# The end of a graph kernel: four tables of sums in HBM are added onto sums in SBUF, by Pool's accumulating transfers instead of loads and adds

## The chip, the cores and the metric

The kernel runs on one core of a Trainium2 chip. The metric is the device time of one execution in microseconds; the time before is the median of three runs. "PE" is TensorE, "DVE" is VectorE, "ACT" is ScalarE, "Pool" is GpSimd and "SP" is SyncE, which here only issues transfers.

## The reference

One layer of a graph network over 6250 nodes with 64 features and 200,000 edges. `h` is the node matrix after a layer norm and a Relu. Each edge makes a message, the messages are summed by their source node, divided by the node's count of edges, and a second small network makes the update:

```python
h = jnp.maximum(_layernorm(x, axis=-1), 0.0)
msg = jnp.concatenate([h[col], edge_attr], axis=1)
msg = jnp.maximum(msg @ W1a + b1a, 0.0) @ W1b + b1b
summed = jax.ops.segment_sum(msg, row, num_segments=x.shape[0])
counts = jax.ops.segment_sum(jnp.ones((row.shape[0],), msg.dtype), row, num_segments=x.shape[0])
agg = summed / jnp.maximum(counts, 1.0)[:, None]
out = jnp.maximum(jnp.concatenate([h, agg], axis=1) @ W2a + b2a, 0.0) @ W2b + b2b
return x + out
```

The kernel moves `W1b` behind the sum (the product `W1b @ W2a` is made once, in `wcq`), so what is summed by node is the Relu of the first layer, 64 numbers and a count of 1: `W` = 65 words a node. With 50 nodes on each of 128 partitions (`NT` = 50) a whole set of sums is 128 x 3250 words, 1625 KB.

## The kernel before

**Two kinds of edges.** Part of the edges goes the "sparse" way: groups of six tiles of 128 edges are combined and written to one of four tables in HBM, `sums[0]` to `sums[3]`, by Pool's indirect accumulating transfers (`scatter`, L626), 650 tiles in all. Tile after tile takes the next table, up to tile `OPEN` = 638; the last twelve take tables 0 and 1 only (`KEPT` = 2), so that tables 2 and 3 are complete early. A scatter waits until the one before it on the same table has landed. The other edges go the "dense" way: PE routes them to buckets and sums them by node (`route`, `sum_nodes`, L1563), and DVE adds each half result from PSUM to `dense` in SBUF (`add_sums`, L1139). The dense sums of a macro step are made in ten adds, each of five columns of nodes, in order from column 0 to 49; the semaphore `summed` counts them over the whole program (230 = 23 macro steps of ten). Only the last ten set when `dense` is final.

**The end before the change.** SP waits until tables 2 and 3 are complete (`table_done`, L532), loads table 3 whole into `xc` (`early_tab`, L533) and table 2 whole into `area` (`tab[2]`, L535). Then it waits for Pool's last scatters (`sums_done`) and for the tenth of the last dense adds, and loads tables 0 and 1 in five chunks of columns (`CHUNKS`, L544), into `tab[0]` and `tab[1]`. DVE adds the early table to `dense` in five adds behind its last dense add (`add_early`, L1147). Pool adds `tab[1]` and `tab[2]` to `tab[0]` turn by turn (L766, L768).

**The turns.** What is left runs in 13 turns (`NTURNS`) of four nodes a partition, 256 words wide. `pipelined` writes the stages of each engine out in an order that is fixed: a stage with lead 3 works on the turn three ahead of the last stage. For a turn DVE adds `dense` to the tables' sum (`add_dense`, L1407), takes the count (`counts`, L1411), its reciprocal (`inverse`, L1416), the mean (`mean_of`, L1422), later the hidden sum (`hidden_sum`, L1429) and the result (`result`, L1433). PE turns the mean (L1689), multiplies it (L1695, L1697), brings the sign of the counts to the other layout (`met_t`, L1704) and makes the output rows (`out_rows`, L1711). ACT copies and applies Relu (L896, L900), makes the sign (`met_rows`, L906) and the bias of nodes that have edges (`base`, L912). SP stores the results in three parts (L563, L564).

The hidden sum waits for `base`, `base` for PE's `met_t`; each engine works in its written order, so that a stage that waits holds up all behind it on its engine.

A general branch of the program serves inputs that don't fit these windows. The profile has no instruction of it.

## Time and profile before

| | us |
|---|---|
| median of three runs | 1448.33 (1445.06 to 1450.76) |
| profiled execution | 1445.55 |
| its span, first to last instruction | 1443.7 |
| PE busy in the span | 1347.3 (93%) |
| DVE busy | 1340.7 (93%) |
| Pool busy | 1107.6 (77%) |
| ACT busy | 858.9 (59%) |

The span lies inside the execution's own time and is 1.85 us shorter. Busy shares are means over the whole span; at the end, from about 1398 us, the picture is another one, and there a timeline (instructions of one engine in order of start, with the idle time before them in brackets and what released them) tells more than a share.

### The profile page before, as it was taken

The page shows a single profiled execution, that of the slowest core. Times are in us where ns is not written, and L with a number is a line of the kernel's source. Part 1 is how long each engine was busy: PE and PEld are TensorE (multiplying, and loading weights), DVE is VectorE, ACT ScalarE, POOL GpSimd, SP SyncE. Part 2 cuts the span into 40 slices and gives each one's busy share as a digit, 9 for nine tenths or more (in the row PEclk, how much of TensorE's full clock was granted, in tenths as well). Part 3 has the DMA queues.
Part 4 walks back from the last instruction along what each step waited for, and adds up shares of the span by engine and source line. Part 5 has one row for each costly group of instructions (what it writes and reads, how often), then busy time and mean ns, then how long its engine had stood idle before and what let it go on. Part 6 is the DMA issues. An engine that isn't in the chain of part 4 may idle for free. (4 is left out here: it accounts for less than half of the span.)

```text
span 1443.7 us, 66451 instructions
## 1 busy us (share of the span) xinstructions
PE 1347.3 (93%) x27502; PEld 1295.7 (90%) x27502; DVE 1340.7 (93%) x4194; ACT 858.9 (59%) x1853; POOL 1107.6 (77%) x737
## 2 busy tenths in 40 slices
PE   1667899999999999999999999999999999999967
PEld 1456899999999999999999999999999999999965
DVE  6889899999999899999999999999999999999877
ACT  2427566666666666666666566656666666666605
POOL 3527888887888878887788868888688887888744
PEclk9589999999999999999999999999999999999989
DMA  7737566776677657776677757776677776767352
GB/s 223 269 70 148 101 117 118 126 124 116 118 127 127 112 113 128 123 133 101 125 126 125 125 103 128 122 128 118 114 131 118 120 127 118 117 122 121 48 146 74
DMA packets 224935, 178.59 MB, mean 124 GB/s; under 512 B 149616, under 2 KB 191726, under 8 KB 223479
## 3 DMA queue, kind: packets, MB, share of 16 engines
q1 hardware_dynamic: 130324, 145.66, 38.2%
q0 software_dynamic: 94304, 28.63, 27.8%
q8 instruction: 218, 3.57, 1.0%
q14 instruction: 89, 0.73, 0.2%
HBM read 140.88 MB, written 33.31 MB: 121 GB/s over the span
## 5 line engine op out<-in xcount | busy, mean ns | idle before, releaser
L626 POOL DMA_INDIRECT sums<-vv,sidx x648 | 1045.3, 1613 | 275.2 <-issue 180.5
L854 ACT ACTIVATE area<-rank_ps 64x392 bf16<-64x392 f32 x1150 | 563.9, 490 | 140.7 <-PE rank_ps L1549 115.3
L1563 PE MATMUL rank_ps<-area 128*128 128x65 bf16 x17250 | 625.6, 193 | 7.1 <-issue 4.1
L1563 PEld LDWEIGHTS rank_ps<-area 128*128 128x128 bf16 x17250 | 597.4, 98 | 23.8 <-issue 10.7
L1549 PE MATMUL rank_ps<-r_d,oh 128*128 128x196 bf16 x4600 | 495.8, 249 | 16.2 <-DVE oh L1117 7.3
L1549 PEld LDWEIGHTS rank_ps<-r_d,oh 128*128 128x128 bf16 x4600 | 380.1, 96 | 29.4 <-issue 8.3
L1132 DVE TENSOR_SCALAR area<-iota,local 128x640 bf16<-128x640 int16 x1150 | 393.2, 406 | 4.1
L1117 DVE TENSOR_SCALAR oh<-iota,rank 128x640 bf16<-128x640 int16 x920 | 310.9, 407 | 7.2 <-PE rank_ps L1549 5.7
L831 ACT ACTIVATE r_d<-z_ps 128x512 f32<-128x512 f32 x247 | 147.6, 597 | 78.4 <-PE z_ps L1519 73.4
L842 ACT ACTIVATE vv<-c_ps 128x396 f32<-128x396 f32 x108 | 54.1, 501 | 226.9 <-PE c_ps L1538 225.2
L1139 DVE TENSOR_TENSOR dense<-rank_ps,dense 128x325 f32<-128x325 f32 x230 | 112.1, 487 | 45.5 <-PE rank_ps L1563 44.9
L1513 PE MATMUL z_ps<-wts,et_d 128*128 128x128 f32 x920 | 132.3, 287 | 0.0
L1085 DVE TENSOR_TENSOR r_s<-r_s 128x384 f32<-128x384 f32 x216 | 119.9, 555 | 3.7
L1074 DVE TENSOR_SCALAR same<-ids_s,srcf 128x128 bf16<-128x128 int16 x648 | 118.6, 278 | 0.0
L1513 PEld LDWEIGHTS z_ps<-wts,et_d 128*128 128x128 f32 x920 | 113.4, 194 | 0.0
L1513 PE MATMUL z_ps<-wts,et_s 128*128 128x128 f32 x648 | 100.3, 291 | 1.2 <-issue 1.0
L1513 PEld LDWEIGHTS z_ps<-wts,et_s 128*128 128x128 f32 x648 | 82.5, 194 | 2.0 <-issue 1.6
L1538 PE MATMUL c_ps<-r_s,same 128*128 128x64 bf16 (+1 forms) x1944 | 81.2, 193 | 2.7 <-issue 1.4
L831 ACT ACTIVATE r_s<-z_ps 128x384 f32<-128x384 f32 x108 | 52.8, 489 | 44.8 <-PE z_ps L1519 43.8
L1538 PEld LDWEIGHTS c_ps<-r_s,same 128*128 128x128 bf16 x1944 | 68.3, 97 | 5.0 <-issue 3.8
L1096 DVE TENSOR_TENSOR r_d<-r_d 128x512 f32<-128x512 f32 x98 | 67.2, 685 | 1.7
L1067 DVE TENSOR_SCALAR hots_s<-ids_s,basew 128x384 bf16<-128x384 int16 x216 | 65.1, 342 | 0.9 <-issue 0.8
(193 smaller groups left out, 769.5 us busy)
## 6 DMA issues: line engine op xcount, KB each, us to landing
ids_s<-ids SPq DMA_DIRECT2D x216, 192.0 KB
et_d<-in_e_t SPq DMA_DIRECT2D x115, 256.0 KB
ids_d<-ids SPq DMA_DIRECT2D x115, 256.0 KB
et_s<-in_e_t SPq DMA_DIRECT2D x108, 192.0 KB
sums<-vv,sidx POOLq DMA_INDIRECT x648
sums<-dense POOLq DMA_DIRECT2D x4, 1657.5 KB
wp_s<-p_table SPq DMA_DIRECT2D x216, 15.8 KB
wp_d<-p_table SPq DMA_DIRECT2D x115, 15.8 KB
```

Source lines behind the costliest of these rows:

```text
L626: nc.gpsimd.indirect_dma_start(out=sums[t][:, :], out_offset=bass.IndirectOffsetOnAxis(ap=index, axis=0), in_=rows, in_offset=None, comput ...
L831: nc.scalar.activation(rows3(kind, g)[:, :, PARTS[r]:PARTS[r] + D], z, ACT.Relu).then_inc(split_ready[kind], 1)
L854: ins = nc.scalar.activation(routed[on, t.div(MACRO).mod(2), first:second + 1:second - first, t.mod(MACRO), :], bank[on, :, :], ACT.Copy)
L1074: ins = nc.vector.tensor_scalar(same[:, g.mod(2), k, :], ids_s[:, g.mod(SR), 0, k * P:(k + 1) * P], srcf[:, column_of(S, g, k):column_of(S ...
L1085: nc.vector.tensor_tensor(r3[S][:, :, PARTS[r + 1]:PARTS[r + 1] + D], r3[S][:, :, at:at + D], halves(S, g)[:, :, at:at + D], ALU.subtract) ...
L1117: ins = nc.vector.tensor_scalar(oh1[:, k, :], iota[:], pos[:, bass.ds(t.value(k * DENSE), 1)], None, ALU.is_equal)
L1132: nc.vector.tensor_scalar(oh2[:, g, :], iota[:], local[:, n.mod(2), g:g + 1], None, ALU.is_equal).then_inc(nodes_ready, 1)
L1139: nc.vector.tensor_tensor(part, l2_ps[h][:, 0:BW], part, ALU.add).then_inc(summed, 1)
L1513: nc.tensor.matmul(z_ps[kind][:, j * P:(j + 1) * P], et[kind][:, slot, j * P:(j + 1) * P], wts[:, C_W1A_BOT:C_W1A_BOT + P], start=j == 0, ...
L1538: t = nc.tensor.matmul(c_ps[b][:, k * R:k * R + n], same[:, b, k, :], halves(S, g)[:, k, PARTS[r]:PARTS[r] + n], start=r == 0, stop=r == 2)
L1549: ins = nc.tensor.matmul(l1_ps[f % 2][:, i * RW:(i + 1) * RW], oh1[:, k, block * P:(block + 1) * P], halves(DN, t)[:, k, :], start=k == si ...
L1563: ins = nc.tensor.matmul(l2_ps[h][:, u * W:u * W + w], oh2[:, g, u * P:(u + 1) * P], rows[:, PARTS[r]:PARTS[r] + w], start=g % MACRO == 0 ...
```

## The change

The tables are no longer loaded. Pool issues 12 direct transfers with an add, each from one table in HBM onto the dense sums in SBUF, for three ranges of columns, `FOLDS` = 0 to 9, 10 to 29 and 30 to 49. The first on a range waits until the dense adds of its columns are done (`summed`), each further one until the one before it on the same range has landed (`folded`). Tables 2 and 3 come first on ranges 0 and 1, then, behind the wait for the last scatters, tables 0 and 1; range 2 takes all four at the end. `total`, from which means and signs are made, is now `dense` itself. DVE takes counts and reciprocals once for a range, at the first turn that touches it: turns 0, 2 and 7. ACT's sign waits for that count instead of for the turn's sum. Chunks, early table, pads, Pool's adds and DVE's adds of tables go.

```diff
-CHUNKS = [(0, 1), (1, 3), (3, 6), (6, 9), (9, NTURNS)]
+FOLDS = [(0, 10), (10, 30), (30, NT)]
...
-        total = tab[0].rearrange("p (t w) -> p t w", w=W)
+        total = dense[:].rearrange("p (t w) -> p t w", w=W)
...
+        def folds_of(m):
+
+            return 1 + next(c for c, (_, last) in enumerate(FOLDS) if min((m + 1) * NPG, NT) <= last)
...
-                sp.wait_ge(table_done, 1)
-                sp.dma_start(early_tab, sums[TABLES - 1][0:REAL, :].rearrange("(p t) w -> p (t w)", t=NT)).then_inc(early_in, 16)
-                sp.wait_ge(summing, done(BUCKETS * (DENSE - MACRO)))
-                sp.dma_start(tab[2][:, 0:NT * W], sums[2][0:REAL, :].rearrange("(p t) w -> p (t w)", t=NT)).then_inc(half_in, 16)
...
+                def fold(t, c, nth):
+
+                    first, last = FOLDS[c]
+                    part = slice(first * W, last * W)
+                    if nth:
+                        pool.wait_ge(folded[c], 16 * nth)
+                    else:
+                        pool.wait_ge(summed, done(PER * DENSE - (NT - last) // UNITS))
+                    pool.dma_start(dense[:, part], sums[t][0:REAL, :].rearrange("(p t) w -> p (t w)", t=NT)[:, part],
+                                   accum_op=ALU.add).then_inc(folded[c], 16)
...
+                    early = range(KEPT, TABLES)
+                    for t in early:
+                        pool.wait_ge(scattered[t], 16 + 16 * len(range(t, OPEN, TABLES)))
+                    for nth, t in enumerate(early):
+                        fold(t, 0, nth)
+                        fold(t, 1, nth)
                     for k in range(KEPT):
                         t, before = table_of(SPARSE * TILES[S] + SPILL - 1 - k)
                         pool.wait_ge(scattered[t], 32 + 16 * before)
+                    for t in range(KEPT):
+                        fold(t, 0, TABLES - KEPT + t)
+                        fold(t, 1, TABLES - KEPT + t)
+                    for nth in range(TABLES):
+                        fold(nth, 2, nth)
...
-                for m in range(NTURNS):
-                    part = bass.ds(m * (NPG * W), NPG * W)
-                    pool.wait_ge(tables_in, done(m + 1))
-                    nc.gpsimd.tensor_tensor(tab[0][:, part], tab[0][:, part], tab[1][:, part], ALU.add).then_inc(pool_part, 1)
-                    pool.wait_ge(pool_part, done(m + 1))
-                    nc.gpsimd.tensor_tensor(tab[0][:, part], tab[0][:, part], tab[2][:, part], ALU.add).then_inc(pool_sum, 1)
...
                 def met_rows(b, m):
-                    act.wait_ge(added, done(m + 1))
+                    act.wait_ge(counts_ready, folds_of(m))
...
                 def counts(b, m):
-                    dve.wait_ge(added, done(m + 1))
-                    nc.vector.tensor_scalar(of(m, 1), total[:, bass.ds(m * NPG, NPG), D], 1.0, None,
-                                            ALU.max).then_inc(counts_ready, 1)
-
-                def inverse(b, m):
-                    dve.wait_ge(counts_ready, done(m + 1))
-                    nc.vector.reciprocal(of(m, 2), of(m, 1)).then_inc(inverse_ready, 1)
+                    for c, (first, last) in enumerate(FOLDS):
+                        if folds_of(m) > c >= (folds_of(m - 1) if m else 0):
+                            last = NTP if last == NT else last
+                            dve.wait_ge(folded[c], 16 * TABLES)
+                            nc.vector.tensor_scalar(stat[:, 1, first:last], total[:, first:last, D], 1.0, None,
+                                                    ALU.max).then_inc(counts_ready, 1)
+                            dve.wait_ge(counts_ready, c + 1)
+                            nc.vector.reciprocal(stat[:, 2, first:last], stat[:, 1, first:last]).then_inc(inverse_ready, 1)
...
-                pipelined([(3, add_dense), (3, counts), (3, inverse), (1, hidden_sum), (3, mean_of), (0, result)])
+                pipelined([(3, counts), (1, hidden_sum), (3, mean_of), (0, result)])
```

Pool's queue, where its last scatters (`sums<-vv,sidx`) end and the branch is left. Before:

```order
L626 DMA sums<-vv,sidx 6528x65 [waits scattered0]
L626 DMA sums<-vv,sidx 6528x65 [waits scattered1]
L626 DMA sums<-vv,sidx 6528x65 [waits scattered0]
L626 DMA sums<-vv,sidx 6528x65 [waits scattered1]
L688 UNCONDITIONAL_BRANCH [waits scattered0,scattered1]
```

Now, with line numbers of the changed program:

```order
L599 DMA sums<-vv,sidx 6528x65 [waits scattered1]
L653 DMA dense<-sums 128x650 [waits summed,scattered3,scattered2]
L653 DMA dense<-sums 128x1300 [waits summed]
L653 DMA dense<-sums 128x650 [waits folded0]
L653 DMA dense<-sums 128x1300 [waits folded1]
L653 DMA dense<-sums 128x650 [waits folded0,scattered0,scattered1]
L653 DMA dense<-sums 128x1300 [waits folded1]
L653 DMA dense<-sums 128x650 [waits folded0]
L653 DMA dense<-sums 128x1300 [waits folded1]
L653 DMA dense<-sums 128x1300 [waits summed]
L653 DMA dense<-sums 128x1300 [waits folded2] x3
L668 UNCONDITIONAL_BRANCH
```

Twelve transfers onto `dense` stand between the last scatter and the end of the branch; Pool's 26 adds behind the branch are gone.

DVE's queue at the start of the turns (`stat` holds counts and reciprocals, `stage` the means and hidden sums). Before:

```order
L1147 TENSOR_TENSOR dense<-dense,xc 128x650 [waits summed] x4
L1400 UNCONDITIONAL_BRANCH
L1439 MEMSET area 128x130 [waits summed]
L1439 MEMSET area 128x130 x2
L1407 TENSOR_TENSOR area<-area,dense 128x260 [waits xb_ready,pool_sum,early_added,pads_ready]
L1411 TENSOR_SCALAR stat<-area 128x4 [waits added]
L1416 RECIPROCAL stat<-stat 128x4 [waits counts_ready]
L1422 TENSOR_TENSOR stage<-area,stat 128x256 [waits at_raw,inverse_ready]
```

Now:

```order
L1371 UNCONDITIONAL_BRANCH [waits summing]
L1380 TENSOR_SCALAR stat<-dense 128x10 [waits folded0,xb_ready,summed]
L1383 RECIPROCAL stat<-stat 128x10 [waits counts_ready]
L1389 TENSOR_TENSOR stage<-dense,stat 128x256 [waits at_raw,inverse_ready] x2
L1380 TENSOR_SCALAR stat<-dense 128x20 [waits folded1]
L1383 RECIPROCAL stat<-stat 128x20 [waits counts_ready]
L1396 TENSOR_TENSOR stage<-z_ps,stage 128x256 [waits res_raw,base_ready,hid_raw]
```

The count of range 1 stands ahead of the first hidden sum. And at the step of turn 7's mean, now:

```order
L1400 TENSOR_TENSOR xc<-c_ps,xs 128x256 [waits res_raw]
L1380 TENSOR_SCALAR stat<-dense 128x22 [waits folded2]
L1383 RECIPROCAL stat<-stat 128x22 [waits counts_ready]
L1396 TENSOR_TENSOR stage<-z_ps,stage 128x256 [waits res_raw,base_ready,hid_raw]
L1389 TENSOR_TENSOR stage<-dense,stat 128x256 [waits at_raw,inverse_ready]
```

The count of range 2 stands ahead of the hidden sum of turn 5, the mean of turn 7 and the result of turn 4. PE's order is unchanged.

## Rows read from the trace of the kernel before

**Rows 1.** The page: span, and busy time by engine with its share.
```profile
span 1443.7 us, 66451 instructions
PE 1347.3 (93%) x27502; PEld 1295.7 (90%) x27502; DVE 1340.7 (93%) x4194; ACT 858.9 (59%) x1853; POOL 1107.6 (77%) x737
```

**Rows 2.** Timeline of DVE, from the last dense adds to turn 2.
```profile
1377.94 0.50 DVE L1139 TENSOR_TENSOR dense<-rank_ps,dense 128x325 f32<-128x325 f32 x1 [1.75 <-PE rank_ps L1563]
...
1388.12 0.48 DVE L1139 TENSOR_TENSOR dense<-rank_ps,dense 128x325 f32<-128x325 f32 x1
...
1397.52 0.50 DVE L1139 TENSOR_TENSOR dense<-rank_ps,dense 128x325 f32<-128x325 f32 x1 [1.78 <-PE rank_ps L1563]
...
1403.92 0.84 DVE L1407 TENSOR_TENSOR area<-area,dense 128x260 f32<-128x260 f32 x1 [1.75 <-POOL area L768]
1404.80 0.58 DVE L1411 TENSOR_SCALAR stat<-area 128x4 f32<-128x4 f32 x1
...
1405.63 0.70 DVE L1422 TENSOR_TENSOR stage<-area,stat 128x256 f32<-128x256 f32 x1
...
1408.07 0.82 DVE L1422 TENSOR_TENSOR stage<-area,stat 128x256 f32<-128x256 f32 x1
...
1411.63 0.52 DVE L1422 TENSOR_TENSOR stage<-area,stat 128x256 f32<-128x256 f32 x1
```

**Rows 3.** Timeline of Pool: start, duration, operation, idle before and releaser.
```profile
1376.02 1.59 POOL L626 DMA_INDIRECT sums<-vv,sidx  x1 [4.61 <-DMA sums<-vv,sidx]
1378.79 1.65 POOL L626 DMA_INDIRECT sums<-vv,sidx  x1 [1.18 <-DMA sums<-vv,sidx]
1380.75 1.57 POOL L626 DMA_INDIRECT sums<-vv,sidx  x1 [0.31 <-issue]
1382.62 1.62 POOL L626 DMA_INDIRECT sums<-vv,sidx  x1 [0.30 <-issue]
...
1389.70 1.63 POOL L626 DMA_INDIRECT sums<-vv,sidx  x1 [0.30 <-issue]
1402.25 0.73 POOL L766 TENSOR_TENSOR area<-area 128x260 f32<-128x260 f32 x1 [10.92 <-DVE area L1439]
```

**Rows 4.** Timeline of all engines: step of turn 7's mean, and one ring later.
```profile
1423.87 0.42 DVE L1429 TENSOR_TENSOR stage<-z_ps,stage 128x256 f32<-128x256 f32 x1
...
1428.42 0.42 DVE L1429 TENSOR_TENSOR stage<-z_ps,stage 128x256 f32<-128x256 f32 x1 [0.44 <-ACT stage L912]
...
1428.88 0.42 ACT L900 ACTIVATE stage<-stage 128x256 f32<-128x256 f32 x1 [0.55 <-DVE stage L1429]
...
1430.02 0.28 PE L1704 MATMUL rank_ps<-ident_b,hots_d 128*128 128x128 bf16 x2
1430.05 0.56 ACT L912 ACTIVATE stage<-rank_ps,wts,wcq 128x256 f32<-128x256 f32 x1
...
1430.70 0.42 DVE L1429 TENSOR_TENSOR stage<-z_ps,stage 128x256 f32<-128x256 f32 x1 [0.44 <-ACT stage L912]
```

**Rows 5.** Timeline of PE in the last sums: idle before them in brackets.
```profile
1376.06 21.42 PE L1563 MATMUL rank_ps<-area 128*128 128x64 bf16 x655 [1.49 <-issue]
```

**Rows 6.** Pool's plain transfers of 128 rows: ns min/median/max of one.
```profile
L593 POOL DMA_DIRECT2D sums<-dense x4: 533/552/838, 24.7 to 26.6; - x4
```

**Rows 7.** SP's ten pieces (L544): issue times, and us from issue to landing.
```profile
L544 SPq DMA_DIRECT2D area<-sums x10: 320/426/568, 1398.1 to 1406.9; - x10
...
DMA to landing us min/median/max: 2.3/3.8/5.3
```

**Rows 8.** Stretches: length, busy by engine, granted clock, DMA share, GB/s moved.
```profile
1372.00:1376.00 4.00, 2.56 (x85) 2.44 (x81) 3.96 (x14) 0.00 (x0) 0.00 (x0) 1.00 1.08 379
1379.00:1388.00 9.00, 8.93 (x274) 8.49 (x271) 7.41 (x24) 0.00 (x0) 6.36 (x5) 1.00 0.29 19
1404.00:1410.00 6.00, 3.05 (x10) 2.29 (x11) 5.76 (x10) 1.10 (x3) 5.69 (x8) 0.50 0.97 330
```

**Rows 9.** DMA issues of the window 1360 to 1444: count, KB each, median us to landing.
```profile
xc<-sums SPq DMA_DIRECT2D x1, 1625.0 KB, 7.2
...
area<-sums SPq DMA_DIRECT2D x4, 390.0 KB, 4.5
```

More of the change, by code:

```diff
@@ L213, in words @@
             return area[0:parts, first:first + n]
-        free = MACRO * BUCKETS * RW // 2 if MACROS % 2 else 0
-        tab = [words(a, NTP * W) for a in ((0 if free else NTP * W), free + (1 if free else 2) * NTP * W, free)]
-        assert NTP * W <= BUCKETS * MACRO * RW // 2
-        early_tab = xc[:].rearrange("p t d -> p (t d)")[:, 0:NT * W]
-        total = tab[0].rearrange("p (t w) -> p t w", w=W)
+        total = dense[:].rearrange("p (t w) -> p t w", w=W)
         n_routed, n_oh2 = MACRO * BUCKETS * RW, BUCKETS * LOCAL // 2
@@ L347, in gnn_kernel @@
         x_in = [sem(f"x_in{k}") for k in range(len(X_PARTS))]
-        sums_in = [sem(f"sums_in{c}") for c in range(len(CHUNKS))]
+        folded = [sem(f"folded{c}") for c in range(len(FOLDS))]
         rows_in = [sem(f"rows_in{r}") for r in range(2)]
@@ L669, in scatter @@
                         scatter_rows(k, t, sidx[:, slot, k:k + 1], vv[:, slot, k, 0:W])
-                        if first + k == OPEN + 3:
-                            for early in range(KEPT, TABLES):
-                                pool.wait_ge(scattered[early], 16 + 16 * len(range(early, OPEN, TABLES)))
-                            pool.sem_inc(table_done, 1)
                     pool.sem_inc(groups_ended, 1)
+                def fold(t, c, nth):
[7 more added lines that the diff above has]
+                                   accum_op=ALU.add).then_inc(folded[c], 16)
                 def gather(at):
@@ L755, in _ @@
                     pool.wait_ge(dsrc_in, 16 * DENSE)
-                    pool.sem_inc(table_done, 1)
-                pool.sem_inc(sums_done, 1)
-                pool.sem_inc(pool_part, START)
-                pool.sem_inc(pool_sum, START)
-                pool.wait_ge(pads_ready, TABLES - 1)
-                pool.wait_ge(half_in, 16)
-                for m in range(NTURNS):
-                    part = bass.ds(m * (NPG * W), NPG * W)
-                    pool.wait_ge(tables_in, done(m + 1))
-                    nc.gpsimd.tensor_tensor(tab[0][:, part], tab[0][:, part], tab[1][:, part], ALU.add).then_inc(pool_part, 1)
-                    pool.wait_ge(pool_part, done(m + 1))
-                    nc.gpsimd.tensor_tensor(tab[0][:, part], tab[0][:, part], tab[2][:, part], ALU.add).then_inc(pool_sum, 1)
+                    for t in range(TABLES):
+                        fold(t, 0, t)
+                        fold(t, 1, t)
+                    for t in range(TABLES):
+                        fold(t, 2, t)
             @block.scalar
@@ L928, in _ @@
                           *zsum_ready, *gidx_ready, slots_ready, local_ready, nodes_ready, summed, dsum_ready, dpick_ready, dsidx_ready,
-                          added, counts_ready, inverse_ready, a_ready, hsum_ready, res_ready):
+                          a_ready, hsum_ready, res_ready):
                     dve.sem_inc(s, START)
@@ L1139, in add_sums @@
                     nc.vector.tensor_tensor(part, l2_ps[h][:, 0:BW], part, ALU.add).then_inc(summed, 1)
-                def add_early(k):
-                    if k == 0:
-                        dve.wait_ge(early_in, 16)
-                    part = slice(k * PER * BW, (k + 1) * PER * BW)
-                    dve.wait_ge(summed, done(PER * (DENSE - MACRO + k + 1)))
-                    nc.vector.tensor_tensor(dense[:, part], dense[:, part], early_tab[:, part], ALU.add).then_inc(early_added, 1)
                 def add_bias():
@@ L1291, in fast @@
                     cycles(cycle)
-                    for m in range(MACRO):
-                        add_early(m)
                 def general():
@@ L1391, in general @@
                     cycles(cycle)
-                    for m in range(MACRO):
-                        add_early(m)
                 fit = dve.value_load(fits_i[0:1, 0:1], min_val=0, max_val=1)
@@ L1437, in _ @@
                 dve.wait_ge(summed, done(PER * DENSE))
-                for k in range(TABLES - 1):
-                    nc.vector.memset(tab[k][:, NT * W:NTP * W], 0.0).then_inc(pads_ready, 1)
-                dve.wait_ge(pads_ready, TABLES - 1)
-                dve.wait_ge(early_added, MACRO)
                 dve.wait_ge(xb_ready, 1)
-                pipelined([(3, add_dense), (3, counts), (3, inverse), (1, hidden_sum), (3, mean_of), (0, result)])
+                pipelined([(3, counts), (1, hidden_sum), (3, mean_of), (0, result)])
             @block.tensor
```

29 lines of the change are left out of this document (3 added, 26 removed).

## The prediction

> **What bounds the kernel now.** I read the page first: in a span of 1443.7 us PE is busy 93% [rows 1], and the change touches none of PE's rows. So the main loop, up to the last sums at about 1398 us, keeps its length, and the question is the last 46 us. There I read the timelines of Pool, DVE and SP. DVE adds the last unit sums to `dense` one bucket at a time: of the last ten adds the second is at 1377.94, the sixth at 1388.12 and the tenth at 1397.52 [rows 2]. SP waits for that tenth add, loads tables 0 and 1 in pieces, Pool adds them from 1402.25 [rows 3], DVE adds `dense` from 1403.92, and the first mean starts at 1405.63 [rows 2]. Then come 13 turns. The chain ahead of the first turn is thus 1405.63 - 1398.02 = 7.6 us; that is all that a faster merge could win before the turns.
>
> What limits a turn? In the last six turns one sum of the hidden layer starts 2.28 us after the other (1428.42, 1430.70) [rows 4]. Behind the first the rows show a ring: DVE's hidden sum, ACT's Relu at 1428.88, PE's last product L1704 at 1430.02, ACT's L912 at 1430.05 for 0.56, DVE again at 1430.70. DVE's table add, count and reciprocal are not on it. In turns 2 to 6 (Pool at work; from turn 2's mean at 1411.63 [rows 2] to turn 7's, 0.34 behind 1423.87 [rows 4], 2.5 us a turn) they nearly are; that is worth at most 0.2 us a turn, and only while the sums are there in time.
>
> **The change part by part.**
> 1. Gone: SP's loads of four tables (two of 1625 KB, then ten pieces), Pool's 26 adds, DVE's five adds of an early table, three memsets, 13 `dense` adds and the per-turn counts and reciprocals. All this ends by 1405.6 or lies beside the ring, so with sums ready it would win the 7.6 us and perhaps 1.2 us of turns 2 to 6. Also gone is the jam of the big loads: Pool's scatters waited 4.61 and 1.18 us in it instead of 0.3 [rows 3]. Without it Pool's last scatter ends at 1391.33 - 4.3 - 0.9 = 1386.1, in time for what follows. PE stood still 1.49 us in the same jam [rows 5]; if that goes too, everything is 1.5 us earlier. I count it at 0, bound 0 to 1.5.
>
> 2. New: 12 accumulating transfers, one behind another for each of three ranges of columns, since all add to the same words. Range 0 (325 KB each) may start when Pool is free, 1386.1. Range 1 (128 x 1300 x 4 B = 665.6 kB, 650 KB in the page's unit) needs the sixth add: 1388.12 + 0.48 = 1388.6 [rows 2]. Range 2 (as large) needs the tenth add, and stands in Pool's order behind the last transfer of range 1. Let a link be the time from one 650 KB transfer to the next: Pool's wake-up, its instruction, the data, the landing. Range 1 has its fourth transfer started at 1388.6 + 3 links; range 2 starts 0.85 us behind it and takes 4 links. So the sums are complete at **1389.45 + 7 links**. Pool's wait for each landing holds up every transfer behind it; DVE's count for range 2 stands ahead of the hidden sum and the result of its step, so DVE, and then PE and ACT, stop for it.
>
> 3. The price of a link. Not the data: Pool's gap before a DMA instruction is 0.30 [rows 3]; its plain DMA of 128 rows is 0.55 [rows 6]; a late scatter was followed by the one that needs it 3.83 us later (1378.79, 1382.62 [rows 3]), so it landed within 3.5 us of its start, of which its instruction is 1.65 and its eight packets per DMA engine some 0.5, which leaves at most 1.35. SP's small pieces land 2.3 us after issue at the least [rows 7], of which 0.35 is data: 1.95 with the issue. So 0.3 + 0.55 + 1.35 to 1.55 is some 2.3, and 3.4 if an accumulating DMA costs Pool as much as a scatter (1.6). I take 2.6. The data: a copy moves at 379 GB/s [rows 8], 665.6 kB in 1.76 us; that is the lower end. Upper end: between the scatters, which are accumulates too, 0.29 of 16 engines moved 19 GB/s, 66 GB/s if all were busy [rows 8]; at that 665.6 kB take 10.1 us. The scatter's packets are of 260 B and reach HBM, those here of 5200 B and go to SBUF, so the copy is the nearer row. But an accumulate has to read `dense` as well as the table, two reads for one write; I take the copy's time twice, 3.5 us. **Link = 2.6 + 3.5 = 6.1 us**, bounds 2.3 + 1.8 = 4.1 and 3.4 + 10.1 = 13.5.
>
> The Trainium skill says the same of sums made in the DMA engines: Collectives: The Full Stack, The bandwidth ceiling, measures a reduce at half the rate of a gather because it needs two source reads. By that rule the data term is the 3.5 us above. No run here shows it yet.
>
> 4. The sum. Sums complete: 1389.45 + 7 x 6.1 = 1432.1; range 0's data shares the engines with range 1's, and range 2's first with range 1's last: I add 1.5 us (bounds 0 and one transfer's 3.5), 1433.6. Count and reciprocal of 22 columns: 0.6 (the count of 4 columns took 0.58 beside Pool's adds [rows 2]; nothing works beside these). The hidden sum that they hold up is that of the step where turn 7's mean is made; its row now is at 1423.87 [rows 4], and from there to the end of the span are 19.8 us, all at 2.28 a turn, so that the removed DVE work shortens nothing. Last, the clock: after PE's gap from 1397.5 [rows 5] to the end of the first mean, 1406.3, the granted clock was 0.50 from 1404 to 1410 [rows 8], and the means of turns 1 and 2 were 3.56 us apart (1408.07, 1411.63 [rows 2]) where those of turns 0 and 1 are 2.44 apart: 1.1 us. The new wait is as long, so I add 1.1. End: 1433.6 + 0.6 + 19.8 + 1.1 = 1455.1, against 1443.7 **11.4 us later**. Range 1 does not decide: it is complete at 1388.6 + 24.4 = 1413, its five turns take 12, and DVE waits for range 2 from about 1425. The profiled execution took 1445.55 (1.85 around its span), which gives 1457.0; the median of the runs is 2.8 higher, 1448.33, which gives 1459.8. I say **1458**.
>
> The break-even link follows: 1389.45 + 7 links + 1.5 + 21.5 = 1443.7 at 4.5 us. A half per cent, 7.2 us, is about what a measurement of this kernel can tell from no change: slower by more than that from a link of 5.5, faster below 3.6 (3.8 if the 1.5 us of PE come in).
>
> **Rivals.**
> A. One pass: the adding is hidden in the copy. The scatters can be read that way: 0.29 of 16 engines over 9 us for five scatters of 128 rows is 65 ns a packet, where a copy at 379 GB/s would move 260 B in 11 [rows 3, 8]. If the other 54 ns are paid per packet and not per byte, a packet of 5200 B costs 219 + 54 ns, eight of them 2.2 us, near the copy's 1.76. Link 2.6 + 1.76 = 4.4; complete at 1420.2 + 0.7 for sharing; end 1442.4, 1.3 us earlier: 1444.2 on the profile's scale, 1447.0 on the median's. No measurable change.
>
> B. Faster: the link is as short as SP's small transfers make it, 2.3 us [rows 7] for 130 KB plus 1.4 for the other 520 KB at 379 GB/s: 3.7 us. Then the sums are complete at 1415.4, with PE's 1.5 us back at 1413.9; end 1413.9 + 21.5 = 1435.4, so 8.3 us earlier: 1437.2, or 1440.0 on the median's scale. It decides below 3.8. Against it: SP's 390 KB pieces, two at a time, took 4.5 us [rows 9], and here Pool's instruction comes on top.
>
> The Trainium skill has a rule with this outcome: DMA: Bandwidth & Descriptors, Anatomy of one DMA, fits 2.0 us + bytes / 436 GB/s to a Pool transfer, which is 3.5 us here, 3.8 with Pool's gap. That fit is for copies; no row shows it for a sum, and the 4.5 us of SP's pieces speak against it.
>
> C. Much slower: descriptors cut small, or a sum that runs at the scatters' rate. Link 13; complete at 1480.5; end 1502, 58 us later: 1506. Only the scatters' packets speak for it; for rows twenty times as long I hold that unlikely, but half that loss is possible (link 9: 1474, 1479 on the median's scale).
>
> **How the numbers follow.** Two passes, link 5.5 to 9: 0.57, time 1458. A: 0.27. B: 0.05. C (over 9): 0.11. Slower by over 0.5%: 0.57 + 0.11 = 0.68; within 0.5%: 0.27; faster: 0.05. The range leaves out most of B and of C: it runs from a link of 4.1 with PE's 1.5 us back (1389.45 + 28.7 + 21.5 - 1.5 = 1438.1, with the 4.6 of the scales 1442.7) to just above a link of 9: 1443 to 1480.
>
> **What would show it.** The twelve transfers in Pool's timeline: starts of range 2's four 6 us apart, the first at about 1407.5; range 1's at 1389, 1395, 1401, 1407. DVE idle from 1398 to its first count at about 1406, some 5 us before the second (1413) and some 8 before the third, at about 1434. PE granted 0.5 after that wait. The turns from there 2.28 us apart. No scatter waits of over 2 us after 1370. Wrong if range 2's links are near 4.4 (A), if the first count comes before 1402 and the wait for range 2 is under 2 us (B), if Pool's instruction alone is over 3 us or links over 9 (C), or if turns come under 2.2 us apart, which would mean that the DVE work was on the ring after all.

## The result, and the profile after

| | before | after |
|---|---|---|
| median of the runs, us | 1447.74 (4 runs, 1445.06 to 1450.76) | 1458.47 (4 runs, 1458.22 to 1460.44) |
| profiled execution, us | 1445.55 | 1460.44 |
| its span, us | 1443.7 | 1458.6 |

The changed kernel takes 1.0084 times as long, 95% interval [1.0067, 1.0102]: slower by 10.7 us. The forecast was 1458. On another chip the same pair gave 1456.42 against 1440.14 us: slower by 16.3 us, ratio 1.0106 [1.0087, 1.0126].

The page of the changed kernel, busy time of each engine (compare [rows 1]):

```profile
PE 1348.9 (92%) x27502; PEld 1297.0 (89%) x27502; DVE 1326.7 (91%) x4153; ACT 860.4 (59%) x1853; POOL 1098.3 (75%) x723
```

The instructions of PE are the same in number. DVE and Pool have fewer, and the kernel is slower, so the loss is in waits. Pool's timeline of the changed kernel shows where (start us, us, engine, line, operation, out<-in, count, idle before and what ended it; L599 is the scatter, L653 the new transfer):

```profile
1380.87 1.56 POOL L599 DMA_INDIRECT sums<-vv,sidx  x1 [0.30 <-issue]
1381.85 1.56 POOL L653 DMA_DIRECT2D dense<-sums  x1
1385.78 0.97 POOL L653 DMA_DIRECT2D dense<-sums  x1 [2.37 <-DVE dense L1122]
1387.90 0.85 POOL L653 DMA_DIRECT2D dense<-sums  x1 [1.15 <-DMA dense<-sums]
1392.30 0.85 POOL L653 DMA_DIRECT2D dense<-sums  x1 [3.55 <-DMA dense<-sums]
1395.63 0.84 POOL L653 DMA_DIRECT2D dense<-sums  x1 [2.48 <-issue]
1398.89 0.85 POOL L653 DMA_DIRECT2D dense<-sums  x1 [2.43 <-DMA dense<-sums]
1400.70 0.84 POOL L653 DMA_DIRECT2D dense<-sums  x1 [0.95 <-DMA dense<-sums]
1405.76 1.74 POOL L653 DMA_DIRECT2D dense<-sums  x2 [4.22 <-DMA dense<-sums]
1416.29 0.86 POOL L653 DMA_DIRECT2D dense<-sums  x1 [8.79 <-DMA dense<-sums]
1423.92 0.84 POOL L653 DMA_DIRECT2D dense<-sums  x1 [6.76 <-DMA dense<-sums]
1430.34 0.85 POOL L653 DMA_DIRECT2D dense<-sums  x1 [5.58 <-DMA dense<-sums]
```

In Pool's order these rows are ranges 0, 1, 0, 1, 0, 1, 0, then ranges 1 and 2 in the row with x2, then range 2 three times. Range 1 starts at 1385.78, 1392.30, 1398.89 and 1405.76: links of 6.5, 6.6 and 6.9 us. Range 2 starts at about 1406.6 (1405.76 and the first instruction's 0.85), then at 1416.29, 1423.92 and 1430.34: links of 9.7, 7.6 and 6.4, and a landing after 6.2. The jam of before is gone: from 1371.58 on, ahead of which one scatter waited 1.04 us, the scatters follow each other after 0.3 us, where they had waited 4.61 and 1.18 [rows 3].

DVE's timeline of the changed kernel: its last dense adds (L1122), the three counts (L1380), and hidden sums (L1396) around the last count (compare [rows 2, 4]):

```profile
1384.99 0.50 DVE L1122 TENSOR_TENSOR dense<-rank_ps,dense 128x325 f32<-128x325 f32 x1
...
1395.15 0.50 DVE L1122 TENSOR_TENSOR dense<-rank_ps,dense 128x325 f32<-128x325 f32 x1 [2.71 <-PE rank_ps L1526]
1407.21 0.17 DVE L1380 TENSOR_SCALAR stat<-dense 128x10 f32<-128x10 f32 x1 [11.57 <-DMA dense<-sums]
...
1412.19 0.18 DVE L1380 TENSOR_SCALAR stat<-dense 128x20 f32<-128x20 f32 x1 [3.76 <-DMA dense<-sums]
...
1422.59 0.42 DVE L1396 TENSOR_TENSOR stage<-z_ps,stage 128x256 f32<-128x256 f32 x1 [1.19 <-issue]
...
1436.58 0.18 DVE L1380 TENSOR_SCALAR stat<-dense 128x22 f32<-128x22 f32 x1 [12.91 <-DMA dense<-sums]
1437.00 0.36 DVE L1396 TENSOR_TENSOR stage<-z_ps,stage 128x256 f32<-128x256 f32 x1
...
1439.46 0.42 DVE L1396 TENSOR_TENSOR stage<-z_ps,stage 128x256 f32<-128x256 f32 x1 [1.44 <-issue]
...
1442.77 0.42 DVE L1396 TENSOR_TENSOR stage<-z_ps,stage 128x256 f32<-128x256 f32 x1 [2.21 <-issue]
...
1445.05 0.42 DVE L1396 TENSOR_TENSOR stage<-z_ps,stage 128x256 f32<-128x256 f32 x1 [1.19 <-issue]
```

DVE stands still three times for the new transfers: 11.57, 3.76 and 12.91 us. The hidden sum held up by the last wait starts at 1437.00; its counterpart in the kernel before is at 1423.87 [rows 4]. That is 13.1 us later, and behind it come 21.6 us to the end of the span where before there were 19.8. Together that is the 14.9 us between the two spans.

The windows of the changed kernel (columns: window, its length, busy time of PE, PEld, DVE, ACT and Pool, the granted clock of PE, the share of the DMA engines, GB/s):

```profile
1405.00:1406.00 1.00, 0.00 (x0) 0.00 (x0) 0.00 (x0) 0.00 (x0) 0.24 (x1) 0.50 1.08 203
...
1430.00:1431.00 1.00, 0.00 (x0) 0.00 (x0) 0.00 (x0) 0.00 (x0) 0.66 (x1) 0.50 0.00 0
1431.00:1432.00 1.00, 0.00 (x0) 0.00 (x0) 0.00 (x0) 0.00 (x0) 0.19 (x1) 0.50 0.66 60
1432.00:1433.00 1.00, 0.00 (x0) 0.00 (x0) 0.00 (x0) 0.00 (x0) 0.00 (x0) 0.50 0.67 68
...
1434.00:1435.00 1.00, 0.00 (x0) 0.00 (x0) 0.00 (x0) 0.00 (x0) 0.00 (x0) 0.50 1.03 208
```

```profile
1437.00:1442.00 5.00, 4.16 (x18) 3.67 (x19) 2.11 (x7) 2.45 (x7) 0.00 (x0) 0.53 0.01 3
1442.00:1450.00 8.00, 7.20 (x45) 5.31 (x43) 3.66 (x11) 5.37 (x14) 0.00 (x0) 1.00 0.38 122
```

They show one link from inside. With all DMA engines busy the sums move at 203 to 208 GB/s, where copies moved at 379 [rows 8]. Nothing moves in the microsecond around Pool's instruction, and for some two more the rate is 60 to 68. After the wait PE is granted 0.53 of its clock in the mean of 5 us, so for most of them half speed (1.2 GHz); from 1442 it has its full 2.4 GHz again.

### The profile page after: what moved, and what is told of

Its sections match the earlier page's. It is cut to its first block and busy times, and to the rows that moved or that the text cites. A ratio compares the mean times of both kernels' runs of the same rounds, so it can differ in the third digit from the quotient of the medians.

```text
span 1458.6 us, 66368 instructions
## 1 busy us (share of the span) xinstructions
PE 1348.9 (92%) x27502; PEld 1297.0 (89%) x27502; DVE 1326.7 (91%) x4153; ACT 860.4 (59%) x1853; POOL 1098.3 (75%) x723
## 5 line engine op out<-in xcount | busy, mean ns | idle before, releaser
L599 POOL DMA_INDIRECT sums<-vv,sidx x648 | 1045.6, 1614 | 265.5 <-issue 184.7
L1115 DVE TENSOR_SCALAR area<-iota,local 128x640 bf16<-128x640 int16 x1150 | 398.0, 410 | 4.1
L1122 DVE TENSOR_TENSOR dense<-rank_ps,dense 128x325 f32<-128x325 f32 x230 | 111.9, 487 | 35.6 <-PE rank_ps L1526 33.4
```

The lines of the kernel that those rows point to most:

```text
L599: nc.gpsimd.indirect_dma_start(out=sums[t][:, :], out_offset=bass.IndirectOffsetOnAxis(ap=index, axis=0), in_=rows, in_offset=None, comput ...
L1115: nc.vector.tensor_scalar(oh2[:, g, :], iota[:], local[:, n.mod(2), g:g + 1], None, ALU.is_equal).then_inc(nodes_ready, 1)
L1122: nc.vector.tensor_tensor(part, l2_ps[h][:, 0:BW], part, ALU.add).then_inc(summed, 1)
```

## The experiments

The theory is a chain that nothing covers: seven links of an accumulating transfer, each 2.6 us of fixed time and two passes of data over the engines. Its rivals are that the adding costs no second pass; that size has little to do with a link; that DVE, PE or the clock set the end and the sums are merely late too; and that the transfers cost the time by what they do to others, wherever they stand. The first four experiments and the repeat of the changed kernel take the chain apart; the five versions after them ask what such transfers cost without it. The first four ran once each, on a chip on which the changed kernel itself did not run. The third, which only adds work of DVE, stands for it there.

### The adding taken out

```diff
-pool.dma_start(dense[:, part], sums[t][0:REAL, :].rearrange("(p t) w -> p (t w)", t=NT)[:, part],
-               accum_op=ALU.add).then_inc(folded[c], 16)
+pool.dma_start(dense[:, part], sums[t][0:REAL, :].rearrange("(p t) w -> p (t w)", t=NT)[:, part]).then_inc(folded[c], 16)
```

> The twelve transfers without the add (plain copies from Pool, same sizes, order and waits; the tables are then not added). If an accumulate costs two passes of data (the prediction's step, and 203 to 224 GB/s at full share in the trace of the changed kernel against 379 for copies before), the undisturbed link of range 2 falls from 6.4 and 6.2 us to about 4.8, seven links fall by some 11 us and the span from 1458.6 to about 1447. If the add is hidden and a Pool transfer is simply slow (rival A's one pass with a dearer fixed part), links stay at 6.2 to 6.4 and the span within 2 us of 1458.6.

Measured: 1435.11 us in one execution, the kernel before beside it 1439.29. Pool's timeline, range 2's last three transfers, and the summary of the line (durations min/median/max in ns):

```profile
1399.35 0.53 POOL L653 DMA_DIRECT2D dense<-sums  x1 [5.39 <-DMA dense<-sums]
1403.96 0.53 POOL L653 DMA_DIRECT2D dense<-sums  x1 [4.08 <-DMA dense<-sums]
1408.21 0.53 POOL L653 DMA_DIRECT2D dense<-sums  x1 [3.73 <-DMA dense<-sums]
```

```profile
L653 POOL DMA_DIRECT2D dense<-sums x12: 527/534/1229, 1373.9 to 1408.2; - x12
...
DMA to landing us min/median/max: 4.0/4.4/5.6
```

The links are 4.6 and 4.25 us, and the last transfer has landed 4.3 after its start, where the sums took 6.4 and 6.2. So the adding costs 2.0 us of a link. Of that 0.3 is Pool's instruction (0.85 against 0.53). The other 1.7 is what one more pass at the copy's rate would take (1.76 us). Two windows of half a microsecond from the copy behind 1408.21 (columns as above) show the rate itself:

```profile
1409.00:1409.50 0.50, 0.50 (x3) 0.45 (x4) 0.14 (x1) 0.27 (x1) 0.00 (x0) 1.00 0.61 89
...
1410.50:1411.00 0.50, 0.50 (x7) 0.49 (x6) 0.00 (x0) 0.33 (x3) 0.00 (x0) 1.00 0.95 395
```

With 0.95 of the engines the copy moves 395 GB/s, the sum with all of them 203 to 208: half. That is the two passes of the forecast, and rival A's one pass is what a copy does. The copy's link begins slowly too (89 GB/s, for about 1 us where the sum has 2), so how the 1.7 us divide between that start and the full rate is not told apart. The span is 20.1 us shorter than that of the third experiment, which adds, on the same chip. From the end of the sixth dense add to the third count it has 35.3 us (1377.2 to 1412.5), the other 51.6 (1379.2 to 1430.8): 16.3 of the 20.1, seven links by 2.0 and some of the data that is shared. Another 1.8 lie behind the third count (20.8 and 22.6 us to the end): 0.4 is the third experiment's extra DVE work ahead of the hidden sum, the rest turns that were slowed there, while here the wait is only 2.05 us and the next turns keep to 2.28; the last 2.0 are the main loop's, which ended earlier by as much in this execution.

The Trainium skill's rule (Collectives: The Full Stack, The bandwidth ceiling) is two source reads and half the rate. The trace agrees on half the rate for these sums into SBUF, 208 against 395 GB/s; the reads themselves no row shows. The Trainium skill's fit for Pool transfers (DMA: Bandwidth & Descriptors, Anatomy of one DMA) gives an estimate of 3.5 us for this size; here even the copy took 4.4 at the median, and the measurement decides.

### Half the columns

```diff
-part = slice(first * W, last * W)
+part = slice(first * W, (first + (last - first) // 2) * W)
```

> Every transfer takes only the first half of its range's columns (the other half of the tables is not added): 325 KB instead of 650. If 3.2 us of the 6.3 us link are data at about 210 GB/s, the undisturbed links fall to about 4.7 and the span to about 1447. If the link is mostly fixed cost, they stay above 5.8 and the span above 1454.

Measured: 1441.86 us, before beside it 1439.29. Pool's timeline, range 2's last three, and DVE's count behind them:

```profile
1404.24 0.86 POOL L653 DMA_DIRECT2D dense<-sums  x1 [5.97 <-DMA dense<-sums]
1409.18 0.84 POOL L653 DMA_DIRECT2D dense<-sums  x1 [4.08 <-DMA dense<-sums]
1414.03 0.85 POOL L653 DMA_DIRECT2D dense<-sums  x1 [4.00 <-DMA dense<-sums]
```

```profile
1418.50 0.18 DVE L1380 TENSOR_SCALAR stat<-dense 128x22 f32<-128x22 f32 x1 [5.03 <-DMA dense<-sums]
```

Links of 4.9, 4.85 and 4.5 us for 325 KB, against about 6.4 for 650. The difference of 1.6 us for 332.8 kB is 208 GB/s, the rate that the windows show. For 650 KB that makes 3.2 us of data and leaves 3.1 to 3.2 fixed. Half the bytes save a quarter of a link: a link is half a fixed price. The span, 1440.0, is 13.4 us below the third experiment's.

### DVE's work put back

```diff
+def old_ops(b, m):
+    part = slice(m * (NPG * W), (m + 1) * (NPG * W))
+    nc.vector.tensor_tensor(words(0, NTP * W)[:, part], total[:, m * NPG:(m + 1) * NPG, :].rearrange("p t w -> p (t w)"), total[:, m * NPG:(m + 1) * NPG, :].rearrange("p t w -> p (t w)"), ALU.add)
+    nc.vector.tensor_scalar(words(NTP * W, NTP)[:, m * NPG:(m + 1) * NPG], stat[:, 1, m * NPG:(m + 1) * NPG], 1.0, None, ALU.max)
+    nc.vector.reciprocal(words(NTP * W + NTP, NTP)[:, m * NPG:(m + 1) * NPG], stat[:, 1, m * NPG:(m + 1) * NPG])
...
-pipelined([(3, counts), (1, hidden_sum), (3, mean_of), (0, result)])
+pipelined([(3, counts), (3, old_ops), (1, hidden_sum), (3, mean_of), (0, result)])
```

> The changed kernel with three DVE instructions put back into every turn, as large as the removed ones (an add of 128x260, a maximum and a reciprocal of 128x4) but writing to unused words. If the ring DVE - ACT - PE - ACT - DVE sets the turn, as the prediction says, turns 9 to 12 stay 2.28 us apart and the span stays within 1 us of 1458.6. If the removed DVE work was on the path, turns come 2.5 to 3 us apart and the span is 3 to 6 us longer.

Measured: 1455.2 us, span 1453.4. The hidden sums (L1402 in this kernel) in DVE's timeline:

```profile
1439.80 0.42 DVE L1402 TENSOR_TENSOR stage<-z_ps,stage 128x256 f32<-128x256 f32 x1 [0.77 <-issue]
...
1442.08 0.42 DVE L1402 TENSOR_TENSOR stage<-z_ps,stage 128x256 f32<-128x256 f32 x1 [0.70 <-issue]
```

They stay 2.28 us apart; only the idle time ahead of each shrinks, from 1.19 to 0.70. What the change takes off DVE in the turns was not on this ring. The instructions put back are the quick ones of a time without Pool: beside Pool's adds, in the kernel before, turns 2 to 6 were 2.5 us apart, and in the changed kernel turns 2 to 4 are 2.28. That gain was had and lost again in the wait behind it. The span is not the 1458.6 of the other chip, but the distance to the kernel before is the same: 15.9 us in one execution each, where the changed kernel has 16.3 on its second chip.

### Range 2 takes two tables

```diff
-for nth in range(TABLES):
+for nth in range(KEPT):
     fold(nth, 2, nth)
...
-dve.wait_ge(folded[c], 16 * TABLES)
+dve.wait_ge(folded[c], 16 * (TABLES if c < 2 else KEPT))
```

> Range 2 takes only two of its four tables (the other two are not added there). If the chain of links sets the end, its last two links (6.4 and 6.2 us) come off: sums complete at about 1424, no third wait of DVE to speak of, and, with PE's clock kept, the span falls by 12 to 14 us to about 1445. If the turns or range 1 set the end, it falls by under 6 us.

Measured: 1442.59 us, span 1440.7. DVE's timeline around the third count:

```profile
1418.06 0.42 DVE L1396 TENSOR_TENSOR stage<-z_ps,stage 128x256 f32<-128x256 f32 x1 [1.19 <-issue]
...
1419.07 0.17 DVE L1380 TENSOR_SCALAR stat<-dense 128x22 f32<-128x22 f32 x1
...
1420.34 0.42 DVE L1396 TENSOR_TENSOR stage<-z_ps,stage 128x256 f32<-128x256 f32 x1 [0.78 <-ACT stage L895]
```

The count is not waited for any more, and the hidden sums stay 2.28 us apart through it. The span is 12.7 us shorter than that of the third experiment on the same chip (1453.4): 0.4 had been won ahead of the wait, 10.9 between the hidden sums of turns 4 and 5 (2.28 apart instead of 13.18), and 1.4 behind them, where the clock's loss is gone with the wait: no turn from 1411.22 on is longer than 2.29. So with four tables the chain of range 2 sets the end. With two the turns set it, not the chain, and that the two missing links had measured 12.6 us together, nearly the whole difference, is in part chance.

### The changed kernel again

> The changed kernel once more, unaltered, on the chip that runs v3_two, so that the experiments have their own base there. By the runs so far 0.8 to 1.1% over the kernel before, sums of range 2 complete about 51 us after its first transfer of range 1 (1379.5 to 1430.7 in e3_dve), undisturbed links of 6.1 to 6.5 us.

Measured: 1456.42 us (4 runs), before 1440.14, ratio 1.0106 [1.0087, 1.0126]. Range 2 in Pool's timeline:

```profile
1402.66 1.74 POOL L653 DMA_DIRECT2D dense<-sums  x2 [3.89 <-DMA dense<-sums]
1413.35 0.86 POOL L653 DMA_DIRECT2D dense<-sums  x1 [8.95 <-DMA dense<-sums]
1419.77 0.84 POOL L653 DMA_DIRECT2D dense<-sums  x1 [5.56 <-DMA dense<-sums]
1426.23 0.85 POOL L653 DMA_DIRECT2D dense<-sums  x1 [5.62 <-DMA dense<-sums]
```

Links of 9.8, 6.4, 6.5 and, to the count at 1432.41, 6.2. The third experiment has 9.8, 6.5, 6.4 and 6.2. The fourth has 9.0 for the first. So a long first link of range 2 is there each time, and the 7.6 of the second in the first profile is not; what stretched that one link by 1.2 us stays open.

### Another place: onto a stock of its own

If the chain is the cost and not the transfers, they should do better on a buffer that is not the last adds' own. Here SP loads table 3 into `xc`, Pool adds tables 2, 0 and 1 onto it in four ranges, and DVE adds the stock to `dense` turn by turn. Nothing waits for a dense add.

```diff
+FOLDS = [(0, 8), (8, 20), (20, 36), (36, NT)]
...
+for pair in range(0, len(FOLDS), 2):
+    for nth, t in enumerate((2, 0, 1)):
+        for c in range(pair, min(pair + 2, len(FOLDS))):
+            fold(t, c, nth)
...
+nc.vector.tensor_tensor(dense[:, part], stock[:, part], dense[:, part], ALU.add).then_inc(added, 1)
```

> A version that keeps the accumulating transfers but takes them off the dense sums: SP loads table 3 into the idle buffer xc early, Pool adds tables 2, 0 and 1 onto xc in four ranges of 8, 12, 16 and 14 columns right behind its last scatter (about 1382 us), and DVE adds xc to the dense sums turn by turn, as before. Three links a range instead of four, and none of them waits for the last dense add at about 1396. If the loss came from the chain standing behind the dense adds, the first range is complete by about 1396, every later one ahead of its turn (1400, 1407, 1416), the first mean starts at 1397 to 1399 and the span is about 1435, 0.5 to 0.8% under the kernel before. If accumulates are too slow altogether (24 us of data at 210 GB/s for three tables, from 1382), the later ranges come late and the span is 1440 to 1450.

Measured: 1445.20 us against 1440.32, ratio 1.0033 [1.0024, 1.0043]. DVE's first table add, and the later one that waits longest:

```profile
1395.97 0.43 DVE L1385 TENSOR_TENSOR dense<-xc,dense 128x260 f32<-128x260 f32 x1 [8.64 <-DMA xc<-sums]
...
1414.82 0.43 DVE L1385 TENSOR_TENSOR dense<-xc,dense 128x260 f32<-128x260 f32 x1 [6.94 <-DMA xc<-sums]
```

About two thirds of the changed kernel's loss are gone (1.0033, against 1.0084 and 1.0106 on other chips), but it is still slower than before, as in the worse case expected. Three transfers on one buffer are still a chain. Pool's waits go in its written order, so the second pair of ranges began only when the first pair's last link could start (1394.54), and DVE stood still for 6.94 us in the middle of the turns.

### Table 2's transfers between the last scatters

```diff
+INTER = (6, 8, 9, 10)
...
+for c in range(len(FOLDS)):
+    if first + k == OPEN + INTER[c]:
+        fold(2, c, 0)
...
-for nth, t in enumerate((2, 0, 1)):
+for nth, t in ((1, 0), (2, 1)):
```

> As v1_stock, but the transfers of table 2 are issued between Pool's last scatters. If Pool and the DMA engines have room there (share 0.29 in that stretch before), the ranges are complete some 4 to 8 us sooner than in v1_stock and the span is equal to it, or up to 2 us shorter where v1 still waits. If the big transfers hold up the scatters behind them, as the loads of the kernel before did by 4.6 us, Pool's last scatter ends later than 1386 and the gain is gone.

Measured: 1440.97 us, ratio 0.9995 [0.9984, 1.0007]: no difference from before, and 4.2 us less than the version above on the same chip. The chain is one link shorter, but the scatters pay. Pool's timeline around the last of them (L609):

```profile
1387.23 1.61 POOL L609 DMA_INDIRECT sums<-vv,sidx  x1 [0.65 <-DMA sums<-vv,sidx]
1393.46 1.82 POOL L670 DMA_DIRECT2D xc<-sums  x2 [4.62 <-DMA sums<-vv,sidx]
```

The transfer that needs the last scatter starts 6.2 us after it. In the version above the same place took 3.8 us (1377.25 to 1381.01), with no large transfer sent between the scatters. So the large ones delay the small one behind them, and table 0's first transfer waits for it.

### No chain at all: two stocks

The early loads of the kernel before stay (table 3 in `xc`, table 2 in `area`). Pool adds table 0 onto the one and table 1 onto the other, in four ranges: eight transfers, none of which waits for another. DVE adds both stocks.

```diff
+for c, (first, last) in enumerate(FOLDS):
+    part = slice(first * W, last * W)
+    for t, stock in enumerate((early_tab, tab[2])):
+        pool.dma_start(stock[:, part], sums[t][0:REAL, :].rearrange("(p t) w -> p (t w)", t=NT)[:, part],
+                       accum_op=ALU.add).then_inc(folded[c], 16)
```

> The kernel before with SP's early loads of table 3 (into xc) and table 2 (into area) kept, and the late loads and all adds of Pool replaced: right behind its last scatters Pool adds table 0 onto xc and table 1 onto area, in four ranges of 8, 12, 16 and 14 columns, so that every range is two transfers side by side and no chain at all. DVE adds both stocks to the dense sums, turn by turn (two adds of 128x260). If the chain of links is what loses, all of it is done by about 1400, no range is waited for, the first mean starts 8 us sooner than in the kernel before and the time is 0.4 to 0.6% under it. With two adds DVE has 2.0 us of work in a ring of 2.28, so turns stay 2.28 us apart; if they come 2.5 apart, 2 to 3 us of the gain go. If the jam of the early loads holds Pool's last scatters up to 1391 as before, the first ranges come late and the gain is under 3 us.

Measured: 1438.19 us against 1440.14 on the same chip, ratio 0.9979 [0.9966, 0.9993]: faster by 2 us, and by 18 than the changed kernel beside it. The expected gain was 0.4 to 0.6%. DVE waits for none of the later ranges. The gain stops at the start; the two rows are the last dense add and the first table add in DVE's timeline:

```profile
1391.03 0.50 DVE L1119 TENSOR_TENSOR dense<-rank_ps,dense 128x325 f32<-128x325 f32 x1 [1.78 <-PE rank_ps L1531]
1396.81 0.43 DVE L1377 TENSOR_TENSOR dense<-xc,dense 128x260 f32<-128x260 f32 x1 [5.28 <-issue]
```

The last dense add ends at 1391.5 and 5.3 us pass for which the profile shows no releaser. The first range had landed by 1394.7, 4.5 and 6.1 us after its two transfers started. Pool's own first transfer comes 5.04 us after its last scatter's instruction, also put down to "issue".

### The same, written inside Pool's branch, and with small first ranges

Pool's eight transfers stood behind the end of a branch of the program. To see whether leaving the branch is what Pool waited for, they go inside it, as `merge`; the last version also cuts the ranges smaller at the front.

```diff
 pool.wait_ge(scattered[t], 32 + 16 * before)
+merge()
```

> v3_two with its eight transfers written at the end of Pool's branch instead of behind it. In v3_two Pool stood still for 5.0 us between its last scatter and the first transfer, against 2.1 in v1_stock, where they are inside the branch, and DVE started its first table add 5.3 us after its last dense add. If leaving the branch costs Pool 3 us, the transfers start 3 us sooner, the first table add follows the last dense add within 3 us and the time is 2 to 3 us under v3_two's (0.3 to 0.4% under the kernel before). If Pool waited for its last scatters to land, nothing moves.

```diff
-FOLDS = [(0, 8), (8, 20), (20, 36), (36, NT)]
+FOLDS = [(0, 4), (4, 12), (12, 28), (28, NT)]
```

> v4_inside with ranges of 4, 8, 16 and 22 columns instead of 8, 12, 16 and 14. If the first table add waits for the first range's data (266 kB on each of two buffers, all eight transfers queued at once), half of that lands about 1.3 us sooner and the time falls by up to 1 us; if DVE's own start is what is late, it stays equal to v4_inside.

Measured: 1442.59 and 1440.88 us against 1444.53, ratios 0.9985 [0.9972, 0.9999] and 0.9965 [0.9952, 0.9978]. Pool's first transfer and DVE's adds in the last version:

```profile
1388.26 0.96 POOL L666 DMA_DIRECT2D xc<-sums  x1 [2.05 <-DMA sums<-vv,sidx]
```

```profile
1394.05 0.50 DVE L1122 TENSOR_TENSOR dense<-rank_ps,dense 128x325 f32<-128x325 f32 x1 [1.78 <-PE rank_ps L1534]
1400.95 0.43 DVE L1380 TENSOR_TENSOR dense<-xc,dense 128x260 f32<-128x260 f32 x1 [6.40 <-issue]
```

Pool's 5.04 us without a releaser became a wait of 2.05 for the scatters (2.03 in the version before it). The other 3 us point to the end of the branch, though the profiles also differ in how the early loads met the scatters. In the total the move inside shows nothing: the intervals of the two versions overlap, and the 2 to 3 us that were expected of it are not there.

With small ranges the kernel is 3.7 us faster than before, the lowest ratio of all that ran, but its interval overlaps those of both other versions. The profiled executions don't show that gain behind the last dense add: from its end to the end of the span are 44.9 us here, 44.1 in the two versions before this one and 45.7 in the kernel before. The rest of the difference lies ahead of it, in the main loop, whose end varies: the last two versions have the same loop, and its last add started at 1397.45 in one execution and at 1394.05 in the other. That small ranges help is not shown.

DVE's gap of 6.40 remains, on the path. DVE does not wait there for its first range. The two transfers of 130 KB landed 3.9 us after their start, by 1392.8, before the last dense add was done; in the version before they landed by 1398.8 and the table add started at 1404.03. What is left is DVE's own way out of its branch. The profile shows three transfers marked "instruction" inside the gap, in full DMA engines, but it shows such transfers elsewhere too and does not say for which engine. Pool's 5.04 us passed before any of the eight transfers was sent, so full engines are not needed for such a gap. In the kernel before, 3.81 us of adds follow the last dense add and DVE's next instruction comes without a gap (1401.71), so there the way out was covered. That the branch's end is the cause is likely and not shown: no run moved DVE's work across it.

## Why the prediction was right

The mechanism is the one forecast. That 1458 lies within a microsecond of the median is luck: the span was forecast 3.5 us too low, at 1455.1 against 1458.6, and the median was expected 2.8 us above the profiled execution, where it came out 2.0 below. On the second chip the loss was 16.3 us, where the forecast had 9.7 (11.4 in the span). Within the span, too, an early start hides a part of what the links cost more, so the terms matter more than the sum.

| step | forecast | measured | difference |
|---|---|---|---|
| sixth dense add ends | 1388.6 | 1385.5 | -3.1 |
| Pool starts behind it | in the link | 0.3 | +0.3 |
| range 1, three links | 18.3 | 20.0 | +1.7 |
| range 2 starts behind range 1's last | 0.85 | 0.85 | 0 |
| range 2, four links, with sharing | 24.4 + 1.5 | 30.0 | +4.1 |
| from there to the span's end | 21.5 | 22.0 | +0.5 |
| span | 1455.1 | 1458.6 | +3.5 |

**The chain.** It is what the forecast said: seven links from the sixth add on, range 2 behind range 1's last transfer in Pool's order, DVE stopped for each count. The fourth experiment removes two links: the wait of DVE is gone, and with it the clock's loss.

**The link.** 6.1 was forecast, and 6.2 to 6.5 are measured where nothing shares the engines. The parts were less good than the sum: fixed 3.1 to 3.2 where 2.6 was taken from small Pool DMAs and SP's landings, data 3.2 where 3.5 was taken. The fixed part was within its own bounds (2.3 to 3.4). Two passes, the step with the widest bounds, is borne out by the copy, which has twice the rate and a link 2.0 us shorter.

**Sharing: the term that was mis-sized most.** I allowed 1.5 us in all. Range 2's first transfer starts 0.85 us behind range 1's last, and both have 3.2 us of data: the later of them lands after the fixed 3.1 and twice 3.2, a link of 9.5, and 9.7 or 9.8 is what three runs have, 9.0 the fourth experiment. That is 3.3 above a link by itself, nearly the 3.5 named as the upper bound. Range 1's three links took 1.1 us more than three by themselves here, and 1.9 to 2.6 in the three other runs with full sums; range 0's transfers lie between them, so their data is the likely reason. Two transfers in flight share one rate (187 to 229 GB/s in all between 1409 and 1412 us), so the whole of the second one's data should have been counted.

**The start and the jam.** The adds came 3.1 us earlier than forecast. But an add at 1335.62 has its counterpart of before at 1337.61, 2.0 earlier, and there neither kernel has any part of the merge. The tenth add is 2.4 us early. At most the remaining 0.4 is the gap that PE had in the jam, of the 1.49 us that I had held possible and counted at zero. A part of it was won by 1385 and lost again: PE has a new gap of 0.77 us at 1393.6, now that sums of ranges 0 and 1 run beside the main loop. Pool's last scatter, forecast to end at 1386.1 when the jam is gone, ended at 1382.4: 2.0 us are the main loop's, and 1.4 a third wait of before, 1.71 us ahead of the scatter at 1387.84, that the forecast left out. But range 1 waited for the sixth add all the same (2.37 us, "DVE dense"), so Pool was early for nothing.

**The waits of DVE.** Forecast: the first count at 1406, then 5 and 8 us of idling, the third count at 1434. Measured: 1407.2, then 3.8 and 12.9, 1436.6. The last wait is longer than forecast because its turns were done by 1423, not 1425, and the sums came 3 us later.

**The turns and the clock.** The ring stays at 2.28 us without DVE's adds, counts and reciprocals, as forecast and as the third experiment shows from the other side. The clock was forecast to cost 1.1 us behind the long wait; the turn from 1439.46 to 1442.77 has 3.31, which is 1.03 more than 2.28, and the one before it 2.46, 0.2 more. Another 0.5 lies behind DVE's last result: from its start (1454.98) to the end of the span are 3.6 us, and 3.1 in the kernel before (1440.63). Count and reciprocal took 0.4 of the 0.6.

**The rivals.** A (one pass, link 4.4) is almost exactly the kernel without the adding, 4.25 to 4.6; on its chip it stood 4 us below before, in one execution. B needed links of under 3.8, which not even 325 KB had. C, a sum that runs at the scatters' rate, fell: the rate is a half of the copy's, not a sixth, and half the bytes in as many rows took half the data time. One sum of the forecast has a slip: its bound of 3.6 for a faster kernel leaves out the 1.5 us of sharing that its break-even of 4.5 counts, and would be 3.4 with it. No link comes near either.

## What to carry to other kernels

An accumulating transfer had a fixed price of 3.1 us here and then moved 208 GB/s, half of what a copy had. Count how many of them must follow each other on the same words behind the last producer, and multiply. The chain of seven took 51 us from the sixth add; the last adds and the first turns ran beside it, and 14.9 us of span were lost. The loads and adds that it replaced took 7.6 us ahead of the first turn. If such sums are used, put them on buffers that are complete early, one transfer for each buffer and range, and let the vector engine join the last terms. Eight transfers so arranged, beside the two early loads, turned a loss of about 1% into a gain of 0.15 to 0.35% in three versions (the best 0.35% [0.22, 0.48]).

## What the runs showed of the hardware that was not expected

- An accumulating transfer costs Pool's own instruction time: 0.85 us against 0.53 for the same one as a copy.
- Each link of the chain begins slowly. After Pool's instruction the rate is 60 to 68 GB/s for about 2 us, with two thirds of the engines' share taken, before it reaches 208. That start is a good part of the fixed 3.1 us, and was no term of the forecast. The copy starts slowly as well, with 89 GB/s for about 1 us.
- Large sums in flight delay a small scatter behind them: the transfer that needs it started 6.2 us after it, against 3.8 where no large one had been sent.
- Behind the end of the main branch DVE stood still 5.3 to 6.4 us, and Pool 5.0 us, in the versions with eight unchained transfers, with no releaser in the profile. Pool's shrank to 2.05 us, a wait for the scatters, when its transfers moved ahead of the branch's end. DVE's was not resolved, but its data had landed 2 us or more before it went on.
